# The causal mask of the score maxima, tiled by query halves: 64x64 instead of 64x128

## Chip, cores and metric

One NeuronCore of a Trainium2 chip runs the whole kernel. The metric is the device time of one execution in microseconds. The kernel before takes 1040.29 us (median of three runs, 1037.0 to 1043.07).

## What is computed

The input x has 16 sequences of 512 tokens with 128 features. Each goes through a layer-normed attention block with 16 heads of 8 features and then a mixture-of-experts feed-forward block. What matters here is the attention:

```
scores = einsum('bhqd,bhkd->bhqk', Qh, Kh)
scores = (scores + einsum('bhqd,qkd->bhqk', Qh, rel_k)) / scale   # rel_k clipped to distance 2
scores = where(causal, scores, -1e9)
attn = softmax(scores)                                            # needs the maximum of each row
out = einsum('bhqk,bhkd->bhqd', attn, Vh) + einsum('bhqk,qkd->bhqd', attn, rel_v)
```

## The kernel before

**Scores twice.** Per sequence and head the kernel forms the scores twice. In the A stage (`s_unit`, `s_part`, L1516) queries stand on the PSUM partitions and keys in the columns; VectorE takes the row maxima (`s_max`, L1127). In the B stage, one step later (`exp_unit` of TensorE, L1493), keys stand on the partitions, the maximum is already subtracted through an extra row, ScalarE applies Exp (L799), GpSimd zeroes what the causal mask forbids (L640), and TensorE multiplies with the values (`av_part`, L1553).

**Steps and rounds.** The attention is a pipeline of 19 steps over four stages: F (layer norm, queries, keys), A (maxima), B (Exp and values), C (output projection and what follows). A step has 20 rounds, r = 0 to 19, in a written order; u = r % 5 picks the shape. In a round TensorE fills two PSUM banks of scores for the maxima, one for each of two heads: `both[1]` by rows 64 to 126 of the array, `both[0]` by rows 0 to 62. With u = 0 or 3 a bank holds one query tile (n = 1, one product of 512 columns); with u = 1, 2 or 4 it holds two (n = 2; 384 + 128 or 256 + 256 columns). Banks come from a ring of three (`s_free`): VectorE reads them in the order `both[1]`, `both[0]`, and each reading frees its bank.

**The mask of the maxima.** Before VectorE may read, the diagonal 128x128 tile of each query tile needs its forbidden columns pushed down. `s_masks` (L1537) does that by products of 64 rows: `below` is a triangle of ones, `masked_at` holds -1e30 in the column that belongs to each row. It issues four matmuls a round, for two parts of the key columns (part 0: the columns of key rows 0 to 63, 64 each; part 1: 65 each) and for the two banks. All have 128 output partitions, that is the tile shape 64*128 of the array, the same as the score products around them. Half of them need the triangle's rows on the other partitions, and take them from a second, rolled copy `below_r`.

**What follows a round.** After the masks, rounds with u = 1, 2, 3 issue `av_part` (tile shape 128*32). The single products and transposes (`AT`) open rounds 1, 2, 5 to 10, 15 and 17 to 19, with shapes 128*128 or 128*32 (one of them 64*128). Only rounds 10, 15 and 19 are followed directly by the next round's score products.

**Start.** GpSimd makes the constants; `masked_columns` (L602) makes the four pieces of `masked_at` in step 0 between `split` and `near_products`. ScalarE makes `below_r` (`roll_halves`, L788). TensorE waits for both at the head of step 1, before a small product at L1741.

Of the kernel before, what the change touches and what calls it, by code (L numbers as in the profile page):

```python
# [8 lines left out]
BF16 = mybir.dt.bfloat16  # L9
U32 = mybir.dt.uint32  # L10
F32R = mybir.dt.float32r
ALU = mybir.AluOpType
# [3 lines left out]
P = 128  # L16
NSEQ, SEQ = 16, 512
# [6 lines left out]
MASKED = -1e30  # L24
HALF = P // 2
# [12 lines left out]
S_UNITS = [[(0, 3, 0)], [(0, 2, 0), (0, 0, 384)], [(0, 1, 0), (1, 1, 256)], [(1, 3, 0)], [(1, 2, 0), (1, 0, 384)]]  # L38
# [184 lines left out]
def block_kernel(nc, x, W_q, b_q, W_k, b_k, W_v, b_v, W_o, b_o, rel_k, rel_v,  # L223
                 router_w, router_bias, sw1, sw3, sw2, ew1, ew2, out):
    ctx = ExitStack()
    with ctx:  # L226
        def sb(name, shape, dt=F32):
            return ctx.enter_context(nc.sbuf_tensor(name, shape, dt))

        def sem(name):  # L230
            return ctx.enter_context(nc.semaphore(name))
# [2 lines left out]
        ident = sb("ident", [P, P])  # L234
        ident16 = sb("ident16", [P, P], F16)
        below = sb("below", [P, P], BF16)
        below_r = sb("below_r", [P, P], BF16)
        masked_at = sb("masked_at", [P, HALF + 1], BF16)
        head_sel = sb("head_sel", [P, D, NPAIR, 2])
        head_sum = sb("head_sum", [P, 32])  # L240
        wq_in = sb("wq_in", [P, P])
# [101 lines left out]
        with ExitStack() as attention:  # L343
# [34 lines left out]


        names = """  # L380
            attn_loaded qk_loaded x_loaded0 x_loaded1 x_loaded2 const_made const_ready rolled bias_full bias_ready
            m_made masked_made v_rows k_rows q_rows
            dve_own pool_own gate_own dve_own2 pool_own2 passed_sp passed_pool passed_dve passed_pe
            s_full s_free0 s_free1 s_free2 e_full e_done misc_full misc_free
# [7 lines left out]
        S = {n: sem(n) for n in names}  # L392
# [10 lines left out]
        N_CONST_MADE, N_POOL_CONST, N_QK_CONST, N_CONST = 11, 6, 6 + 6, 6 + 10  # L403
# [157 lines left out]
        def _(pool):  # L561
# [16 lines left out]
            for m in (ident, ident16):  # L578
                pool.affine_select(out=m[:, :], in_=m[:, :], compare_op=ALU.not_equal, fill=1.0, base=0,
                                   pattern=[[-1, P]], channel_multiplier=1).then_inc(S["const_ready"], 1)  # L580

            pool.affine_select(out=below[:, :], in_=below[:, :], compare_op=ALU.is_ge, fill=0.0, base=0,
                               pattern=[[-1, P]], channel_multiplier=1).then_inc(S["const_ready"], 1)

            for half in range(2):
                v = head_sel[:, :, 4 * half:4 * half + 4, :]
                pool.affine_select(out=v, in_=v, compare_op=ALU.not_equal, fill=1.0, base=-32 * half,
                                   pattern=[[-4, D], [-1, NPAIR // 2], [-64, 2]],
                                   channel_multiplier=1).then_inc(S["const_ready"], 1)

            pool.affine_select(out=m_col[:, :], in_=m_col[:, :], compare_op=ALU.not_equal, fill=-M_UNIT,
                               base=-M_ROW, pattern=[[0, 2]], channel_multiplier=1).then_inc(S["m_made"], 1)
            pool.wait_ge(S["m_made"], 1)
            pool.affine_select(out=m_col[:, :], in_=m_col[:, :], compare_op=ALU.not_equal, fill=-M_UNIT,
                               base=-M_ROW - HALF, pattern=[[0, 2]], channel_multiplier=1).then_inc(S["const_ready"], 1)

            def masked_columns():

                for i, (base, columns) in enumerate(((0, slice(0, HALF)), (-HALF, slice(0, HALF)),
                                                     (1 - HALF, slice(HALF, HALF + 1)), (1 - P, slice(HALF, HALF + 1)))):  # L600
                    v = masked_at[:, columns]
                    pool.affine_select(out=v, in_=v, compare_op=ALU.not_equal, fill=MASKED, base=base,  # L602
                                       pattern=[[-1 if i < 2 else 0, v.shape[1]]],
                                       channel_multiplier=1).then_inc(S["masked_made"], 1)
                    pool.wait_ge(S["masked_made"], i + 1)

            def selectors():

# [153 lines left out]
        def _(act):  # L762
# [19 lines left out]
                        act.dma_start(ks0[lo:lo + D, 0:NPAIR // 2, :],  # L782
                                      part[HALF * b:HALF * b + 32, :]).then_inc(stacks[0][0], 16)

            def roll_halves():

                act.wait_ge(S["const_ready"], N_POOL_CONST)
                act.copy(below_r[0:HALF, :], below[HALF:P, :]).then_inc(S["rolled"], 1)  # L788
                act.copy(below_r[HALF:P, :], below[0:HALF, :]).then_inc(S["rolled"], 1)

            def exp_unit(st, i):
                g, u, b = i // (2 * NU), i % (2 * NU) // 2, i % 2
                n, bank = st.e_use(f"e{i}")

                act.wait_ge(S["e_full"], n + 1)
                if i % (2 * NU) == 0:

                    need(act, S["av_full"], st.at(NGRP * st.b + g - 1, NGRP))
                act.activation(prob[g % 2][:, u, b, :], ps_e[bank][:, :], ACT.Exp,  # L799
                               scale=SCALE).then_inc(S["e_done"], 1)  # L800
# [94 lines left out]
            def gates_out(early):  # L895
# [9 lines left out]
                else:  # L905
                    act.wait_ge(S["gates_stored"], 32)
                    rest = (NSEQ - EARLY) * NE * NT
                    act.copy(gate_sb[0:rest, 0, :], ps_misc[0:rest, 0:P]).then_inc(S["gateT_copied"], 1)

            roll_halves()  # L910

            def step(st):
                def exps(lo, hi):
# [554 lines left out]
        def _(pe):  # L1468
# [47 lines left out]
                pe.matmul(scores[:, at:at + P * (qt + 1)], qs[par][rows, 2 * g + off, P * qt:P * qt + P],  # L1516
                          ks[par][rows, 2 * g + off, 0:P * (qt + 1)], start=(n == 0), stop=False)

            def diagonals(bank, u, part):

                n = len(S_UNITS[u])
                apart = SEQ // 2 if u == 2 else P
                if part == 0 and u != 2:
                    blocks = bank[:, SEQ - 1 - n * P:SEQ - 1].rearrange("p (n c) -> p n c", n=n)
                    return blocks[:, :, 0:HALF]
                blocks = bank[:, SEQ - n * apart:SEQ].rearrange("p (n c) -> p n c", n=n)
                at = apart - HALF - 1 if part else apart - P - 1
                return blocks[:, :, at:at + HALF + part]

            def s_masks(u, both):  # L1530

                n = len(S_UNITS[u])
                for part in range(2):
                    for b in (1, 0):
                        rows = slice(HALF * b, HALF * b + HALF)
                        columns = masked_at[rows, 0:HALF + part].unsqueeze(1).to_broadcast([HALF, n, HALF + part])
                        last = pe.matmul(diagonals(both[b], u, part), (below if b == part else below_r)[rows, :],  # L1537
                                         columns, start=False, stop=(part == 1))
                        if part == 1:
                            last.then_inc(S["s_full"], 1)  # L1540

            def av_part(st, s, g, kt):
# [68 lines left out]
            def s_tok_transpose(st):  # L1611
                m = misc(st, "s_tok")

                pe.sem_inc(passed["pe"], 1)
                transposes(lambda i: m[:, i * 64:i * 64 + 64], lambda i: s_rows[:, i * P:i * P + P],
                           ident[0:64, 0:64], S["misc_full"])
# [110 lines left out]
            def step(st):  # L1727

                uses = {"av2": lambda: av_transpose(st, st.c, 2), "e_sums": lambda: e_sums(st),
                        "m1": lambda: m_transpose(st, st.b, 1), "s_tok": lambda: s_tok_transpose(st),  # L1730
                        "av3": lambda: av_transpose(st, st.c, 3), "v0": lambda: values(st),
                        "oT": lambda: o_transpose(st), "xT": lambda: x_transpose(st), "oproj": lambda: o_proj(st),
                        "q": lambda: queries(st), "k": lambda: keys(st), "av0": lambda: av_transpose(st, st.b, 0),
                        "m0": lambda: m_transpose(st, st.a, 0), "av1": lambda: av_transpose(st, st.b, 1),
                        "xn2": lambda: xn2_transpose(st), "logits": lambda: logits(st)}
                if st.t0 == 1:
                    pe.wait_ge(S["const_ready"], N_CONST)
                    pe.wait_ge(S["rolled"], 2)
                    pe.wait_ge(S["masked_made"], 4)

                    pe.matmul(ps_av[:, 0:P], bias_v[:, :], wo[:, :], start=True, stop=True).then_inc(S["bias_full"], 1)  # L1741
                if st.t0 == 2:
                    pe.wait_ge(S["bias_ready"], 1)
                here = {"F": st.F, "A": st.A, "B": st.B, "C": st.C}
                if st.t0 == NSEQ + 2:
                    gate_transposes(True)
                for r in range(ROUNDS):
                    g, u = r // NU, r % NU
                    for what, use in uses.items():
                        if AT[what] == r and here[STAGE[what]]:  # L1750
                            if st.t0 == NSEQ + 2 and what == "xn2":
                                first_units(st)
                            use()
                    both = [None, None]

                    if st.B:
                        exp_unit(st, 2 * r)
                    if st.A:
                        both[1] = s_unit(st, 2 * r)
                    if st.B:  # L1760
                        exp_unit(st, 2 * r + 1)
                    if st.A:
                        both[0] = s_unit(st, 2 * r + 1)
                        for n in range(1, len(S_UNITS[u])):
                            for i in range(2):
                                s_part(st, 2 * r + i, both[1 - i], n)
                        s_masks(u, both)
                    for kt in {1: (0,), 2: (1, 2,), 3: (3,)}.get(u, ()):
                        if g > 0 and st.B:
                            av_part(st, st.b, g - 1, kt)  # L1770
                        if g == 0 and st.C:
                            av_part(st, st.c, NGRP - 1, kt)
# [43 lines left out]
```

## Time and profile before

| what | value |
| --- | --- |
| runs | 1037.0, 1040.29, 1043.07 us |
| profiled execution | 1038.87 us, span 1037.1 us |
| PE busy in the span | 907.4 us (87%) |
| DVE busy | 834.9 us (80%) |
| POOL, ACT busy | 726.3 us, 678.6 us |
| mean granted TensorE clock | 0.953 of 2.4 GHz |

PE is TensorE's matmuls, PEld its weight loads, DVE VectorE, ACT ScalarE, POOL GpSimd, SP the queue that issues most transfers. A matmul's record starts when it starts to stream its columns; its end is modelled and lies well after the last column, so a pause between two matmuls can be real where the records overlap. The difference of starts is what to read.

### The profile page before, as it was taken

The numbers are of one execution on the slowest core, as the hardware profiler recorded it, in microseconds if no ns is written. First come the engines' busy times: TensorE is split into PE (matmuls) and PEld (weight loads), VectorE is DVE, ScalarE is ACT, GpSimd is POOL, SyncE is SP. The second block draws the span as 40 slices with busy tenths as digits, with TensorE's granted clock in tenths as the row PEclk, the third lists the DMA queues.
The fourth block names the chain that finished last, engine by engine and source line by source line (L and its number), as shares of the span: only waits on it lengthen the run. The fifth ranks groups of instructions, "written<-read, shape, count | busy, mean of one in ns | idle before, by whom it ended". The sixth has DMA issues, their size and how long they took to land. (4 is left out here: it accounts for less than half of the span.)

```text
span 1037.1 us, 23478 instructions
## 1 busy us (share of the span) xinstructions
PE 907.4 (87%) x7655; PEld 519.9 (50%) x7655; DVE 834.9 (80%) x1948; ACT 678.6 (65%) x1305; POOL 726.3 (70%) x940
## 2 busy tenths in 40 slices
PE   2768899999999899999998999987679999999995
PEld 0324444444444444454444444432357777777773
DVE  5677878888888888888888888886568788878884
ACT  2137677767786777777867776765447767676763
POOL 4135676966867868668678686576257989898886
PEclk8569999999999999999999999998979999999999
DMA  2610111101101101011011010102415454554541
GB/s 50 168 45 28 37 39 34 51 33 41 46 32 45 43 33 48 31 43 47 32 45 43 32 49 32 42 13 57 149 58 169 143 165 151 171 148 167 162 139 31
DMA packets 64004, 74.93 MB, mean 72 GB/s; under 512 B 10032, under 2 KB 39600, under 8 KB 63904
## 3 DMA queue, kind: packets, MB, share of 16 engines
q1 hardware_dynamic: 61536, 73.17, 22.2%
q8 instruction: 56, 0.92, 0.4%
q10 hardware_dynamic: 2368, 0.48, 0.3%
q14 instruction: 44, 0.36, 0.1%
HBM read 43.75 MB, written 8.65 MB: 51 GB/s over the span
## 5 line engine op out<-in xcount | busy, mean ns | idle before, releaser
L1127 DVE TENSOR_REDUCE mx<-ps_s 128x1 f32<-128x512 f32 (+2 forms) x640 | 409.3, 684 | 82.3 <-PE ps_s L1537 80.5
L799 ACT ACTIVATE prob<-ps_e 128x512 f32<-128x512 f32 x640 | 347.8, 601 | 121.6 <-PE ps_e L1493 121.6
L640 POOL TENSOR_SCALAR_AFFINE_SELECT prob<-prob 128x516 f32<-128x516 f32 (+1 forms) x320 | 174.0, 568 | 171.3 <-ACT prob L799 171.3
L1516 PE MATMUL ps_s<-ks,qs 63*128 63x512 f16 (+3 forms) x1024 | 215.5, 311 | 20.6 <-DMA ks<-kl 8.6
L1493 PE MATMUL ps_e<-qs,ks 64*128 64x512 f16 (+3 forms) x1024 | 196.3, 304 | 15.8 <-DMA qs<-mT 7.8
L1553 PE MATMUL ps_av<-prob,vp 128*32 128x512 f32 (+3 forms) x2048 | 183.8, 455 | 22.7 <-POOL prob L640 22.4
L721 POOL TENSOR_TENSOR hidden_low<-hidden,hidden_high 128x512 fp32r<-128x512 f32 x144 | 191.2, 1356 | 12.1 <-ACT hidden_high L988 10.8
L1493 PEld LDWEIGHTS ps_e<-qs,ks 64*128 64x128 f16 x1024 | 60.9, 95 | 116.8 <-ACT prob L799 63.9
L988 ACT CAST hidden_high<-hidden 128x512 fp32r<-128x512 f32 x160 | 98.3, 614 | 30.4 <-DVE hidden L1440 25.8
L1537 PE MATMUL ps_s<-masked_at,below_r 64*128 64x130 bf16 (+3 forms) x640 | 106.5, 211 | 0.0
L1516 PEld LDWEIGHTS ps_s<-ks,qs 63*128 63x128 f16 x1024 | 63.6, 95 | 78.0 <-DVE mx L1127 54.5
L1537 PE MATMUL ps_s<-masked_at,below 64*128 64x128 bf16 (+3 forms) x640 | 92.8, 211 | 0.0
L1440 DVE TENSOR_TENSOR hidden<-gate_rows,ps_e 128x512 f32<-128x512 f32 x96 | 64.2, 684 | 28.7 <-ACT ps_e L1004 28.5
L1553 PEld LDWEIGHTS ps_av<-prob,vp 128*32 128x32 f32 x2048 | 47.3, 109 | 69.8 <-POOL prob L640 29.8
L1703 PE MATMUL ps_av<-hidden_high,w_high 128*128 128x512 f32 x160 | 69.3, 433 | 11.6 <-POOL hidden_low L721 11.6
L1004 ACT ACTIVATE ps_e<-ps_e 128x512 f32<-128x512 f32 x96 | 55.8, 582 | 20.5 <-PE ps_e L1670 19.8
L1537 PEld LDWEIGHTS ps_s<-masked_at,below_r 64*128 64x128 bf16 x640 | 60.2, 97 | 16.9 <-issue 1.6
L1703 PE MATMUL ps_av<-hidden_high,w_low 128*128 128x512 f32 x160 | 63.1, 394 | 0.0
L1703 PE MATMUL ps_av<-hidden_low,w_high 128*128 128x512 f32 x160 | 63.0, 394 | 0.0
L1537 PEld LDWEIGHTS ps_s<-masked_at,below 64*128 64x128 bf16 x640 | 53.1, 97 | 13.2 <-issue 0.5
L1561 PEld LDWEIGHTS ps_misc<-ident,av_s 128*128 128x128 f32 x256 | 28.3, 147 | 49.4 <-issue 47.2
L622 POOL TENSOR_TENSOR rs<-var,neg_half 128x4 f32<-128x4 f32 x48 | 49.1, 1024 | 3.8
(176 smaller groups left out, 1738.4 us busy)
## 6 DMA issues: line engine op xcount, KB each, us to landing
gate_rows<-gates_dram SPq DMA_DIRECT2D x128, 256.0 KB, 3.6
qs<-qh SPq DMA_DIRECT2D x128, 32.0 KB
qs<-ql SPq DMA_DIRECT2D x128, 32.0 KB
xnT_dram<-oT SPq DMA_DIRECT2D x16, 256.0 KB, 2.0
xeT<-xnT_dram SPq DMA_DIRECT2D x16, 256.0 KB, 2.7
out<-result SPq DMA_DIRECT2D x16, 256.0 KB, 2.3
v_near<-v_back SPq DMA_DIRECT2D x16, 254.0 KB
ks<-kh SPq DMA_DIRECT2D x124, 32.0 KB
```

The lines of the kernel that those rows point to most:

```text
L640: pool.affine_select(out=v, in_=v, compare_op=ALU.is_ge, fill=0.0, base=-2, pattern=cols, channel_multiplier=-1).then_inc(S["p_masked"], 1)
L721: pool.tensor_tensor(hidden_low[hid(f, i)][:, :].bitcast(F32R), hidden[hid(f, i)][:, :], hidden_high[hid(f, i)][:, :], ALU.subtract).then_ ...
L799: act.activation(prob[g % 2][:, u, b, :], ps_e[bank][:, :], ACT.Exp, scale=SCALE).then_inc(S["e_done"], 1)
L988: act.copy(hidden_high[hid(f, i)][:, :].bitcast(F32R), hidden[hid(f, i)][:, :]).then_inc(S["high_ready"], 1)
L1004: act.activation(front[k % 4][:, :], front[k % 4][:, :], ACT.Gelu).then_inc(S["act_ready"], 1)
L1127: dve.tensor_reduce(out, src, AX.X, ALU.max).then_inc(s_free[bank], 1)
L1440: dve.tensor_tensor(hidden[hid(f, i)][:, :], gate_rows[:, k, :], front[k % 4][:, :], ALU.mult).then_inc(S["hidden_ready"], 1)
L1493: last = pe.matmul(scores[:, at:at + WIDTH[kt]], ks[par][rows, pr, P * kt:P * kt + P], qs[par][rows, pr, P * kt:SEQ], start=True, stop=True)
L1516: pe.matmul(scores[:, at:at + P * (qt + 1)], qs[par][rows, 2 * g + off, P * qt:P * qt + P], ks[par][rows, 2 * g + off, 0:P * (qt + 1)], st ...
L1537: last = pe.matmul(diagonals(both[b], u, part), (below if b == part else below_r)[rows, :], columns, start=False, stop=(part == 1))
L1553: last = pe.matmul(ps_av[32 * j:32 * j + 32, P * kt:SEQ], vp[par][:, kt, 4 * g + j, :], prob[g % 2][:, u, j % 2, at:at + w], start=(kt == ...
L1703: last = pe.matmul(ps_av[:, :], ws[:, w, :].bitcast(F32R), hs[hd][:, :].bitcast(F32R), start=(i % n == 0 and j == 0), stop=(i % n == n - 1 ...
```

## The change

The four mask matmuls of a round are now cut by query halves, not by key columns. Each has 64 rows and 64 output partitions (tile shape 64*64). For the query half 64 to 127 (part 1, issued first) 65 columns a tile are written. For the half 0 to 63 (part 0) all 129 columns from the one before the tile to its last are written, 257 or 258 where the bank has two tiles. All four weights are the diagonal quadrants `below[rows, rows]`, so `below_r`, its two copies on ScalarE and the semaphore `rolled` go. `masked_at` grows from 65 to 257 columns, made by six affine selects in place of four.

```diff
-        below_r = sb("below_r", [P, P], BF16)
-        masked_at = sb("masked_at", [P, HALF + 1], BF16)
+        masked_at = sb("masked_at", [P, 2 * P + 1], BF16)
...
-                for i, (base, columns) in enumerate(((0, slice(0, HALF)), (-HALF, slice(0, HALF)),
-                                                     (1 - HALF, slice(HALF, HALF + 1)), (1 - P, slice(HALF, HALF + 1)))):
-                    v = masked_at[:, columns]
-                    pool.affine_select(out=v, in_=v, compare_op=ALU.not_equal, fill=MASKED, base=base,
-                                       pattern=[[-1 if i < 2 else 0, v.shape[1]]],
-                                       channel_multiplier=1).then_inc(S["masked_made"], 1)
-                    pool.wait_ge(S["masked_made"], i + 1)
+                blocks = masked_at[:, 1:].rearrange("p (n c) -> p n c", n=2)
+                parts = ((masked_at[:, 0:1], 0, [[0, 1]]),
+                         (blocks[:, :, 0:HALF - 1], 1, [[0, 2], [-1, HALF - 1]]),
+                         (blocks[:, :, HALF - 1:], HALF - 1, [[0, 2], [0, HALF + 1]]))
+                made = 0
+                for v, row, pattern in parts:
+                    for b in range(2):
+                        pool.affine_select(out=v, in_=v, compare_op=ALU.not_equal, fill=MASKED, base=-row - HALF * b,
+                                           pattern=pattern, channel_multiplier=1).then_inc(S["masked_made"], 1)
+                        made += 1
+                        pool.wait_ge(S["masked_made"], made)
...
-            def roll_halves():
-
-                act.wait_ge(S["const_ready"], N_POOL_CONST)
-                act.copy(below_r[0:HALF, :], below[HALF:P, :]).then_inc(S["rolled"], 1)
-                act.copy(below_r[HALF:P, :], below[0:HALF, :]).then_inc(S["rolled"], 1)
...
-                for part in range(2):
+                for part in (1, 0):
+                    queries = slice(HALF * part, HALF * part + HALF)
                     for b in (1, 0):
                         rows = slice(HALF * b, HALF * b + HALF)
-                        columns = masked_at[rows, 0:HALF + part].unsqueeze(1).to_broadcast([HALF, n, HALF + part])
-                        last = pe.matmul(diagonals(both[b], u, part), (below if b == part else below_r)[rows, :],
-                                         columns, start=False, stop=(part == 1))
-                        if part == 1:
+                        blocks = both[b][queries, SEQ - n * apart:SEQ].rearrange("p (n c) -> p n c", n=n)
+                        if part:
+                            out = blocks[:, :, apart - HALF - 1:]
+                            columns = masked_at[rows, 0:HALF + 1].unsqueeze(1).to_broadcast([HALF, n, HALF + 1])
+                        elif u == 2:
+                            out = blocks[:, :, apart - P - 1:]
+                            columns = masked_at[rows, 0:P + 1].unsqueeze(1).to_broadcast([HALF, n, P + 1])
+                        else:
+                            out, columns = both[b][queries, SEQ - n * P - 1:SEQ], masked_at[rows, 0:n * P + 1]
+                        last = pe.matmul(out, below[rows, rows], columns, start=False, stop=True)
+                        if part == 0:
                             last.then_inc(S["s_full"], 1)
...
-                    pe.wait_ge(S["rolled"], 2)
-                    pe.wait_ge(S["masked_made"], 4)
+                    pe.wait_ge(S["masked_made"], 6)
```

## Rows read from the trace of the kernel before

**Rows 1.** The page's first part: busy time of each engine, share of the span, instructions.

```profile
PE 907.4 (87%) x7655; PEld 519.9 (50%) x7655; DVE 834.9 (80%) x1948; ACT 678.6 (65%) x1305; POOL 726.3 (70%) x940
```

**Rows 2.** Busy time in four consecutive steps, 443.0 to 608.0 us, summed.

```profile
sum 165.00, PE 153.03 PEld 76.70 DVE 144.66 ACT 121.09 POOL 122.04; mean PE 38.26 PEld 19.17 DVE 36.16 ACT 30.27 POOL 30.51
```

**Rows 3.** Who waited for the mask matmuls of L1537, whole run: us, times.

```profile
  DVE mx L1127: 80.5, 116
```

**Rows 4.** Waits, 443.0 to 484.3 us (one step): engine, line, releaser: us, times, longest.

```profile
DVE mx L1127 <- PE ps_s L1537: 3.7, 7, 0.8
...
PEld ps_s L1516 <- DVE mx L1127: 3.0, 10, 0.4
...
PE ps_av L1553 <- POOL prob L640: 1.5, 2, 0.9
```

**Rows 5.** Groups by form, 200 to 600 us: the mask matmuls, n = 2, then n = 1.

```profile
L1537 PE MATMUL ps_s<-masked_at,below_r 64*128 64x130 bf16 x117 | 25.4, 217 | 0.0
...
L1537 PE MATMUL ps_s<-masked_at,below_r 64*128 64x65 bf16 x78 | 14.7, 188 | 0.0
```

**Rows 6.** Timeline of PE around a mask, n = 1: start us, us, instruction, tile, shape.

```profile
409.13 0.38 PE L1493 MATMUL ps_e<-qs,ks 64*128 64x512 f16 x1
409.34 0.19 PE L1537 MATMUL ps_s<-masked_at,below 64*128 64x64 bf16 x1
...
409.37 0.19 PE L1537 MATMUL ps_s<-masked_at,below 64*128 64x65 bf16 x1
...
409.49 0.42 PE L1553 MATMUL ps_av<-prob,vp 128*32 128x128 f32 x8
409.85 0.33 PE L1493 MATMUL ps_e<-qs,ks 64*128 64x384 f16 x1
```

**Rows 7.** Timeline of the weight loads in the same stretch.

```profile
409.12 0.10 PEld L1537 LDWEIGHTS ps_s<-masked_at,below 64*128 64x128 bf16 x1
...
409.49 0.16 PEld L1553 LDWEIGHTS ps_av<-prob,vp 128*32 128x32 f32 x8
```

**Rows 8.** Timeline of PE from round 19 into round 0 of the next step.

```profile
484.12 0.22 PE L1537 MATMUL ps_s<-masked_at,below 64*128 64x130 bf16 x1
484.16 0.37 PE L1493 MATMUL ps_e<-qs,ks 64*128 64x512 f16 x1
...
485.12 0.39 PE L1516 MATMUL ps_s<-ks,qs 63*128 63x512 f16 x1
485.12 0.20 PE L1537 MATMUL ps_s<-masked_at,below_r 64*128 64x64 bf16 x1
...
485.38 0.19 PE L1537 MATMUL ps_s<-masked_at,below_r 64*128 64x65 bf16 x1
```

**Rows 9.** Timeline of PE in round 4, n = 2.

```profile
451.79 0.22 PE L1537 MATMUL ps_s<-masked_at,below 64*128 64x130 bf16 x1
...
451.95 0.22 PE L1537 MATMUL ps_s<-masked_at,below_r 64*128 64x130 bf16 x1
452.10 0.39 PE L1561 MATMUL ps_misc<-ident,m 128*8 128x128 f16 x4
```

**Rows 10.** Timeline of DVE, rounds 18 and 19 (in brackets idle before, releaser).

```profile
482.36 1.29 DVE L1127 TENSOR_REDUCE mx<-ps_s 128x1 f32<-128x512 f32 x2 [0.15 <-PE ps_s L1537]
...
484.37 1.91 DVE L1127 TENSOR_REDUCE mx<-ps_s 128x4 f32<-128x512 f32 x3 [0.72 <-PE ps_s L1537]
```

**Rows 11.** Timeline of PE: the queries of round 9, and the values after round 16.

```profile
461.62 1.13 PE L1576 MATMUL ps_e<-xnT,wq 128*128 128x512 f32 x2
...
477.08 1.06 PE L1553 MATMUL ps_av<-prob,vp 128*32 128x512 f32 x8 [0.87 <-POOL prob L640]
```

**Rows 12.** Start of the kernel: POOL's timeline.

```profile
19.29 1.29 POOL L602 TENSOR_SCALAR_AFFINE_SELECT masked_at<-masked_at 128x64 bf16<-128x64 bf16 x4
```

**Rows 13.** Waits, 0 to 90 us.

```profile
PE ps_s L1516 <- DMA ks<-kl: 8.6, 2, 8.3
...
PE ps_av L1741 <- POOL masked_at L602: 5.1, 1, 5.1
```

More of the change, by code:

```diff
@@ L380, in block_kernel @@
         names = """
-            attn_loaded qk_loaded x_loaded0 x_loaded1 x_loaded2 const_made const_ready rolled bias_full bias_ready
+            attn_loaded qk_loaded x_loaded0 x_loaded1 x_loaded2 const_made const_ready bias_full bias_ready
             m_made masked_made v_rows k_rows q_rows
@@ L908, in gates_out @@
                     act.copy(gate_sb[0:rest, 0, :], ps_misc[0:rest, 0:P]).then_inc(S["gateT_copied"], 1)
-            roll_halves()
             def step(st):
@@ L1517, in s_part, with s_masks @@
                           ks[par][rows, 2 * g + off, 0:P * (qt + 1)], start=(n == 0), stop=False)
-            def diagonals(bank, u, part):
+            def s_masks(u, both):
                 n = len(S_UNITS[u])
                 apart = SEQ // 2 if u == 2 else P
[L1523 to L1532, printed above, removed]
-                for part in range(2):
+                for part in (1, 0):
+                    queries = slice(HALF * part, HALF * part + HALF)
                     for b in (1, 0):
                         rows = slice(HALF * b, HALF * b + HALF)
-                        columns = masked_at[rows, 0:HALF + part].unsqueeze(1).to_broadcast([HALF, n, HALF + part])
-                        last = pe.matmul(diagonals(both[b], u, part), (below if b == part else below_r)[rows, :],
-                                         columns, start=False, stop=(part == 1))
-                        if part == 1:
+                        blocks = both[b][queries, SEQ - n * apart:SEQ].rearrange("p (n c) -> p n c", n=n)
[9 more added lines that the diff above has]
+                        if part == 0:
                             last.then_inc(S["s_full"], 1)
```

## The prediction

> **What bounds the kernel now.** I read the page's busy times first, then the busy time by stretches, the waits, and last the timeline of single rounds. TensorE is busy for 87% of the span and VectorE for 80% [rows 1]; the mask runs only in the attention, whose middle repeats in steps of 165.00 / 4 = 41.3 us with TensorE busy 38.3 and VectorE 36.2 [rows 2]. Neither is full, and each waits for the other: in one step VectorE waits 7 times, 3.7 us in all, for a mask, and the score products wait 10 times, 3.0 us, for VectorE to free a bank [rows 4]. Over the run VectorE waits 116 times for a mask [rows 3], about 7 in each of the 16 steps that have one. So the end is set by a chain that changes between the two, and the last thing TensorE does before handing over is exactly what is changed.
>
> **Columns.** Two matmuls on different row halves run side by side: in a round with n = 1 the mask pairs start at 409.34 and 409.37 [rows 6]. A column takes 1/2.4 ns (512 of them lie between 409.13 and 409.34 [rows 6]). Before, each row half streams 64 + 65 = 129 columns (54 ns) with n = 1 and 128 + 130 = 258 (107 ns) with n = 2 [rows 5]. After, the longer of the two query halves streams 129 and 257 or 258. If both column halves of the array run side by side, too, as the four 128*32 tiles do (eight matmuls of 128 two-pass columns in 0.42 us, where in a row they would need 8 x 0.107 = 0.85 us [rows 6]), the time is the same: 0. If they run one after the other, it is 27 ns a round more for n = 1 and 54 for n = 2. I take 0.
>
> **The change of tile shape.** This is the term that counts. Score products and masks share the shape 64*128. Between them there is no pause: the mask starts at 409.34, when the 512 columns end, its weights loaded at 409.12 under the products [rows 6, 7]; and from round 19 to 0 the next product starts at 484.16, before the 130 columns of 484.12 have ended [rows 8]. Where the shape changes, there is a pause each time: the last mask at 409.37 has streamed by 409.40, and the 128*32 tiles begin at 409.49, their weights at 409.49 too, not earlier [rows 6, 7]; in round 4 the last mask, 451.95 + 0.05, is followed at 452.10 [rows 9]. That is 0.09 to 0.10 us in which nothing is loaded ahead. No row shows 64*128 followed by 64*64. Bounds: 0, if a mere column split of the same row halves isn't a new shape; 0.12, the pause with a first weight load exposed. Between 64*128 and 128*8 both dimensions differ, so the rows alone leave this open; I take 0.09, because every change in the rows shows it.
>
> Here the Trainium skill has a rule: TensorEngine Tiling (Array Packing), Key Properties, says that changing the tiling mode, not just the tile, drains the engine, and the section Tiling Modes lists 64×128 and 64×64 as different modes. The pauses of 0.09 to 0.10 us agree with a drain. By it the pause is sure and the lower bound of 0 falls away.
>
> To the entry comes the first weight load, which is no longer hidden. The nearest row is the 128*32 block: 0.42 us less two times 0.107 of columns and less the modelled tail of 0.16 (a 64-column mask has 0.19 for 0.03 of columns) leaves 0.04, some 0.02 of it the stagger of eight starts [rows 6]. So 0.02, between 0 and 0.04.
>
> The same skill page, Restrictions and Gotchas, says that column tiling disables the fast weight load. By it, and by the page TensorE: Matmul & The Clock Gate, section LDWEIGHTS (columns over 1.2 GHz), the 64 columns of a mask would take an estimated 53 ns, and each entry 0.03 us more than I take; no run here shows it.
>
> One mask block then costs 0.09 + 0.02 = 0.11 us on entry. On exit 17 of the 20 rounds change shape already; in rounds 10, 15 and 19 the product that now starts at once (484.16 [rows 8]) gets a second pause of 0.09. TensorE's own bill is 20 x 0.11 + 3 x 0.09 = 2.5 us a step, 40 us for 16 steps: the upper bound for side-by-side columns.
>
> **How much of it reaches the end.** I follow one step's waits.
> - Rounds 17 to 19: TensorE leads, VectorE waits before 482.36 (0.15 us) and 484.37 (0.72 us) [rows 10], and once in round 17. Three blocks, all exposed.
> - Rounds 0 and 1: VectorE works without a pause (three reductions from 484.37), and one would say that it covers TensorE. But the bank of `both[0]` is free only after the first reduction, 484.37 + 0.68 = 485.05; its product starts at 485.12 [rows 8, 10]. Before, the masks of `both[1]` ran beside that product (485.12 [rows 8]) and were early. Now all masks wait until the product has drained: 485.12 + 0.21 + 0.11 + 0.05 = 485.49, and VectorE starts 0.20 after the last mask (484.12 + 0.05 to 484.37), at 485.69. It would be free at 484.37 + 2 x 0.61 = 485.59 (reductions start 0.61 apart: 1.91 less 1.29 [rows 10]). So the cover is gone and some 0.1 us is exposed here as well.
> - Rounds 2 to 8: the score products wait for VectorE and VectorE again for masks, in turn, several of the 7 and 10 waits of [rows 4]. Seven blocks, exposed at about 0.11 each.
> - Rounds 9 to 16: from the queries' product at 461.62 a longer chain runs over ScalarE's Exp and GpSimd's masking, and TensorE stands idle 0.87 us before 477.08 [rows 4, 11]. Eight entries and two exits, 8 x 0.11 + 2 x 0.09 = 1.06 us, find 0.87 of cover; 0.2 is left.
> Sum: 12 blocks x 0.11 = 1.3, and 0.2, makes 1.5 us a step; x 16 = 24 us.
>
> **The rest.** The two copies of `below_r` go from ScalarE's start, the affine selects become six, by the four of 1.29 us about 0.65 more, up to 1 us, as they are wider [rows 12]. Behind them on GpSimd stand the `near_products` of step 0, and TensorE's small product waits for them (5.1 us [rows 13]). But after it TensorE waits 8.3 us for the keys' transfers [rows 13], which neither of these moves. 0; with that cover gone, +1. The feed-forward part isn't touched.
>
> The profiled execution takes 1038.87 us; 1038.87 + 24 = 1063. The median of the runs is 1.4 above it. I forecast 1064 us.
>
> **The rivals.**
> - *VectorE covers most* (0.13). The shape costs what I say, but is exposed only where VectorE waits for a mask now: 7 x 0.11 x 16 = 12 us, 1052. For it: VectorE has work queued in rounds 0 to 7. Against: the bank cycle above.
> - *The column halves also stream one after the other, or the weight load is slow* (0.14). Extra 8 x 27 + 12 x 54 ns = 0.86 us a step; on 12 of 20 rounds 0.5 us, x 16 = 8 us, 1072; with everything exposed 40 + 14 = 54 us, 1094. For it: in no row are there two 64-wide column tiles. Against: the 128*32 tiles.
> - *No pause between 64*128 and 64*64* (0.10), the other side. The masks cost the same columns, the shape costs nothing on entry, and four quadrants load less: half the weight columns. Price: 0, or a gain up to 15 ns a block, 320 x 0.015 = 5 us where the loads were late; 1035 to 1041. It decides if the mask block starts when the last product's columns end. For it: only row changes may matter. Against: a pause at every change of shape in the trace. That the change doesn't do what it says would look the same, 1040.
> - My own forecast has 0.63, its own range 1054 to 1075.
>
> **Numbers.** About 0.5% (5 us) is what can be told from no change. The slower cases are 0.63 + 0.13 + 0.14 = 0.90; the no-pause case divides into 0.06 same and 0.04 faster. The range 1049 to 1081 leaves out the no-pause case and the extreme of the second rival.
>
> **What would show it.** Right: 64*64 masks starting about 0.09 us after the products' last column, with their loads not earlier; all four within 0.03 us of each other; no mask beside a product of the other bank; in rounds 10, 15 and 19 a pause before the next product; a step of 42.8 us; VectorE waiting more often, rounds 0 and 1 included; the idle time before 477.08 nearly gone. Wrong: masks that begin at once (no pause), column halves that start 0.05 to 0.11 us apart (second rival), or a step that grows by under 0.9 us though the pause is there (first rival).

## The result and the profile after

The changed kernel takes 1072.28 us (median of four runs, 1056.98 to 1075.88) against 1041.68. The ratio is 1.023, with a 95% interval of 1.018 to 1.028; it counts the two slowest runs of the changed kernel, 1074.09 and 1075.88 us, as slow ones and leaves them out, and so lies below the ratio of the medians, 1.029. In a second comparison it was 1069.99 us (six runs) against 1038.70 (eleven), ratio 1.029, 1.027 to 1.032. The profiled execution took 1070.47 us; its span is 1068.8, 31.7 more than before.

The page's first part and its row of granted clock, by slices of the span:

```profile
PE 966.5 (90%) x7655; PEld 500.5 (47%) x7655; DVE 840.2 (79%) x1948; ACT 680.6 (64%) x1303; POOL 725.2 (68%) x942
...
PEclk8569999999998898988989889898879999999999
```

TensorE is busier by 59 us with the same number of matmuls, its weight loads by 19 us less, and the other engines are within 6 us of before [rows 1]. And there is something the prediction does not mention: through the attention the row of the clock is broken by 8s.

**The pause.** The timeline of PE after the change in round 18 (n = 1), to be held against [rows 6], and of its weight loads, against [rows 7]:

```profile
409.74 0.38 PE L1488 MATMUL ps_e<-qs,ks 64*128 64x512 f16 x1
410.05 0.25 PE L1531 MATMUL ps_s<-masked_at,below 64*64 64x65 bf16 x4
410.23 0.43 PE L1546 MATMUL ps_av<-prob,vp 128*32 128x128 f32 x8
```

```profile
410.05 0.11 PEld L1531 LDWEIGHTS ps_s<-masked_at,below 64*64 64x64 bf16 x4 [0.43 <-issue]
410.23 0.16 PEld L1546 LDWEIGHTS ps_av<-prob,vp 128*32 128x32 f32 x8
```

The 512 columns end at 409.74 + 0.21 = 409.95 and the masks start at 410.05, their weights loaded then and not under the products. The pause is there. The four masks start within 0.03 us of each other (the four records span 0.25 us). From the masks to the 128*32 tiles it is 0.18 us. The 129 columns take 0.05 of it. With two tiles in a bank, here in round 19, it is 0.24 us, of which the longer half's 257 columns take 0.11 (the row names the other half's 130):

```profile
238.26 0.30 PE L1531 MATMUL ps_s<-masked_at,below 64*64 64x130 bf16 x4
238.50 0.39 PE L1488 MATMUL ps_e<-qs,ks 64*128 64x512 f16 x1
```

Both times 0.13 us is left beside the longer half's columns, though the columns double. If the column halves streamed one after the other, the remainder would be 0.10 and 0.08. So they run side by side. The 0.13 holds the stagger of the four starts, the pause and some 0.025 us more than on leaving a 64*128 block. I put this 0.025 down to the masks' first weight load, which no row shows by itself.

**The step.** A step is read from VectorE's first reduction of round 19 to the next such one. The kernel before has it at 484.37 us [rows 10], and one step earlier at 443.06, which makes a step of 41.31 us:

```profile
443.06 0.69 DVE L1127 TENSOR_REDUCE mx<-ps_s 128x4 f32<-128x512 f32 x1 [0.72 <-PE ps_s L1537]
```

In the changed kernel these are the rows at the two ends of a step at full clock, and of one later in the run:

```profile
238.60 0.69 DVE L1122 TENSOR_REDUCE mx<-ps_s 128x4 f32<-128x512 f32 x1 [0.84 <-PE ps_s L1531]
...
281.13 2.04 DVE L1122 TENSOR_REDUCE mx<-ps_s 128x4 f32<-128x512 f32 x3 [0.84 <-PE ps_s L1531]
...
457.39 1.29 DVE L1122 TENSOR_REDUCE mx<-ps_s 128x4 f32<-128x512 f32 x2 [1.39 <-PE ps_s L1531]
...
501.77 1.29 DVE L1122 TENSOR_REDUCE mx<-ps_s 128x4 f32<-128x512 f32 x2 [1.39 <-PE ps_s L1531]
```

The first two are 42.53 us apart, 1.22 more than before; the last two 44.38. The three reductions that took 1.91 us without a pause [rows 10] now take 2.04: the 0.13 us is the gap in round 0 that the prediction expected, because a bank is freed too late. The 44.38 has another cause, shown by the busy time and granted clock (the number before the DMA share) in stretches cut at the changes of the clock:

```profile
core 0: us, PE busy (x) PEld busy (x) DVE busy (x) ACT busy (x) POOL busy (x), PEclk, DMA share, GB/s
...
329.60:367.10 37.50, 36.08 (x372) 16.08 (x364) 31.50 (x78) 26.22 (x51) 26.11 (x37) 1.00 0.10 34
367.10:373.90 6.80, 6.80 (x42) 2.15 (x45) 4.81 (x14) 4.13 (x11) 4.38 (x9) 0.50 0.15 51
373.90:411.40 37.50, 36.09 (x372) 15.99 (x364) 31.52 (x78) 26.23 (x51) 26.01 (x37) 1.00 0.10 34
411.50:418.30 6.80, 6.80 (x42) 2.15 (x45) 4.81 (x14) 4.13 (x11) 4.38 (x9) 0.50 0.14 50
```

From 322.8 us on the clock falls to 1.2 GHz for 6.8 us in every step, always from round 19 to the values behind round 1, each time costing 44.38 - 42.53 = 1.85 us. There are nine such falls in the attention's steps, about 17 us. The kernel before had one fall of 3.4 us in the same stretch.

The rest can be counted in steps. In both kernels the third of these reductions comes at nearly the same time, and the last one 13 steps later, first before and then after the change:

```profile
153.65 1.91 DVE L1127 TENSOR_REDUCE mx<-ps_s 128x4 f32<-128x512 f32 x3 [0.72 <-PE ps_s L1537]
...
688.79 1.29 DVE L1127 TENSOR_REDUCE mx<-ps_s 128x4 f32<-128x512 f32 x2 [0.72 <-PE ps_s L1537]
```

```profile
153.27 2.04 DVE L1122 TENSOR_REDUCE mx<-ps_s 128x4 f32<-128x512 f32 x3 [0.84 <-PE ps_s L1531]
...
721.32 1.29 DVE L1122 TENSOR_REDUCE mx<-ps_s 128x4 f32<-128x512 f32 x2 [0.84 <-PE ps_s L1531]
```

That is 535.1 against 568.1 us: 32.9 more, of which 13 x 1.22 = 16 are the pauses and 17 the clock. So the growth of the span alone would mislead: the two shares have to be told apart. And up to 153 us the changed kernel lost nothing in these two executions, though it had the pauses there as well. The kernel before had three falls of the clock of 3.4 us between 80 and 150 us, the changed kernel one; whether that is the whole reason was not tried.

### The profile page after: what moved, and what is told of

It reads as the page before. It is cut to its first block and busy times, and to the rows that moved or that the text cites. A ratio compares the mean times of both kernels' runs of the same rounds, so it can differ in the third digit from the quotient of the medians.

```text
span 1068.8 us, 23480 instructions
## 1 busy us (share of the span) xinstructions
PE 966.5 (90%) x7655; PEld 500.5 (47%) x7655; DVE 840.2 (79%) x1948; ACT 680.6 (64%) x1303; POOL 725.2 (68%) x942
## 5 line engine op out<-in xcount | busy, mean ns | idle before, releaser
L1122 DVE TENSOR_REDUCE mx<-ps_s 128x1 f32<-128x512 f32 (+2 forms) x640 | 414.0, 683 | 104.1 <-PE ps_s L1531 95.9
L1511 PE MATMUL ps_s<-ks,qs 63*128 63x512 f16 (+3 forms) x1024 | 227.0, 323 | 20.6 <-DVE mx L1122 9.3
L1488 PE MATMUL ps_e<-qs,ks 64*128 64x512 f16 (+3 forms) x1024 | 204.3, 317 | 6.5 <-DMA qs<-mT 3.4
L1511 PEld LDWEIGHTS ps_s<-ks,qs 63*128 63x128 f16 x1024 | 67.0, 97 | 89.1 <-DVE mx L1122 62.9
L1531 PE MATMUL ps_s<-masked_at,below 64*64 64x130 bf16 (+4 forms) x1280 | 95.2, 263 | 0.0
L1531 PEld LDWEIGHTS ps_s<-masked_at,below 64*64 64x64 bf16 x1280 | 37.1, 106 | 89.9 <-issue 87.3
L1554 PE MATMUL ps_misc<-ident,av_s 128*128 128x128 f32 x256 | 43.3, 294 | 4.0 <-ACT av_s L861 3.9
L1696 PEld LDWEIGHTS ps_av<-hidden_high,w_high 128*128 128x128 f32 x160 | 30.3, 189 | 31.3 <-POOL hidden_low L724 27.2
```

Of the source, the lines that this page charges most:

```text
L1122: dve.tensor_reduce(out, src, AX.X, ALU.max).then_inc(s_free[bank], 1)
L1488: last = pe.matmul(scores[:, at:at + WIDTH[kt]], ks[par][rows, pr, P * kt:P * kt + P], qs[par][rows, pr, P * kt:SEQ], start=True, stop=True)
L1531: last = pe.matmul(out, below[rows, rows], columns, start=False, stop=True)
L1554: last = pe.transpose(dst(i), src(i), unit)
L1696: last = pe.matmul(ps_av[:, :], ws[:, w, :].bitcast(F32R), hs[hd][:, :].bitcast(F32R), start=(i % n == 0 and j == 0), stop=(i % n == n - 1 ...
```

## The experiments

Steps below are read as above, at full clock where not said. Every ratio is against the kernel before, run beside it: 1038.70 us in experiments 1 to 3, 1040.82 in 4, 5 and the first of 6, 1039.76 in the second of 6 and in 7. Experiments 1 to 3 ran on one chip, 4 to 7 on another.

**1. The changed kernel again, six runs.**

> The changed kernel itself, to see how its time goes with the clock. Theory A (two costs: a pause at each change of tile shape, and TensorE's clock falling to 1.2 GHz for 6.8 us in most steps): runs in which the clock stays at 2.4 GHz take about 1057 us at a mean clock of 0.95, runs with the falls 1070 to 1076 at 0.93. Theory B (the clock has no part, all of the loss is the pauses): the time doesn't go with the clock.

Measured (us at mean granted clock): 1063.83 at 0.949, 1064.04 at 0.950, 1069.54 at 0.928, 1070.45 at 0.929, 1071.03 at 0.926, 1073.45 at 0.923; the four runs of the first comparison: 1056.98 at 0.952, 1070.47 at 0.929, 1074.09 at 0.925, 1075.88 at 0.931. On the whole the time goes with the clock, which speaks for theory A and against B. But at a mean clock of 0.95 this set took 1064, not the expected 1057: the profile of the run with 1064.04 us shows seven of the falls of 6.8 us, where that of the first comparison has nine.

**2. 64*64 masks in a part of the rounds.** Both kinds of mask are kept, and the round chooses:

```diff
-                        s_masks(u, both)
+                        (s_masks_new if 9 <= r <= 16 else s_masks_old)(u, both)
```

(in the second run `not 9 <= r <= 16`)

> 64*64 masks in rounds 9 to 16 alone, 64*128 in the others (below_r kept, masked_at made by six selects). By the prediction's split the idle time before the values of round 16 covers them: +0.2 us a step, +3 us, 1043 to 1045. If every pause counts (rival): 8 x 0.11 + 2 x 0.09 = 1.06 a step, +17 us, 1057.

> 64*64 masks in rounds 17 to 19 and 0 to 8 alone. By the prediction 12 x 0.11 = 1.3 us a step, +21 us, about 1061, without a fall of the clock; if VectorE covered rounds 0 to 8, 3 x 0.11 x 16 = +5, 1046. If the clock falls here too, up to 1072; that would place its cause in these rounds.

Rounds 9 to 16 alone: 1046.14 us, ratio 1.007 (1.005 to 1.009), little falling of the clock. The others alone: 1057.68, ratio 1.018 (1.014 to 1.021), with falls in some steps. Two consecutive steps of each, at full clock:

```profile
486.29 1.91 DVE L1131 TENSOR_REDUCE mx<-ps_s 128x4 f32<-128x512 f32 x3 [0.72 <-PE ps_s L1541]
...
528.24 1.90 DVE L1131 TENSOR_REDUCE mx<-ps_s 128x4 f32<-128x512 f32 x3 [0.71 <-PE ps_s L1541]
```

```profile
280.53 2.04 DVE L1131 TENSOR_REDUCE mx<-ps_s 128x4 f32<-128x512 f32 x3 [0.84 <-PE ps_s L1563]
...
322.53 2.04 DVE L1131 TENSOR_REDUCE mx<-ps_s 128x4 f32<-128x512 f32 x3 [0.84 <-PE ps_s L1563]
```

41.95 and 42.00: +0.64 and +0.69 a step. Together they make 1.33, near the change's whole 1.22, but the split is not the predicted one of 0.2 and 1.3. Rounds 9 to 16 cost three times as much, the others half.

**3. Half of the columns.** The query half 0 to 63 also gets 65 columns a tile, so that the longer column half streams half of what it did. The kernel then leaves out the mask of the key columns 64 to 127 for these queries.

```diff
-                        elif u == 2:
-                            out = blocks[:, :, apart - P - 1:]
-                            columns = masked_at[rows, 0:P + 1].unsqueeze(1).to_broadcast([HALF, n, P + 1])
                         else:
-                            out, columns = both[b][queries, SEQ - n * P - 1:SEQ], masked_at[rows, 0:n * P + 1]
+                            at = apart - P - 1 if u == 2 else apart - HALF - 1
+                            out = blocks[:, :, at:at + HALF + 1]
+                            columns = masked_at[rows, 0:HALF + 1].unsqueeze(1).to_broadcast([HALF, n, HALF + 1])
```

> The changed kernel with only 65 columns a tile for the query half 0 to 63 as well (the upper key half stays unmasked, left out on purpose of cost): same 1280 matmuls, same shapes, half of the mask's columns. If the shape is the cost, the steps shorten by at most the columns, 27 ns (n = 1) or 54 ns (n = 2) a round, 0.4 to 0.9 us a step, and remain over the kernel before by 0.5 us or more a step; if the columns are the cost (the rival of halves one after the other), the step falls to about that of before, 41.3.

1052.61 us, ratio 1.014 (1.011 to 1.017); steps of 42.18 us (reductions at 534.32 and 576.50). With half the columns the masks in 64*64 still cost 0.87 us a step over the kernel before. So most of the cost is the shape's; halving the columns gives back 0.35 us a step of the 1.22.

**4. Each bank's masks behind its own products.** The same edit on both kernels (`s_masks` gets the banks as a third argument; that part is not shown):

```diff
                     if st.A:
                         both[1] = s_unit(st, 2 * r)
+                        for n in range(1, len(S_UNITS[u])):
+                            s_part(st, 2 * r, both[1], n)
+                        s_masks(u, both, (1,))
                     if st.B:
                         exp_unit(st, 2 * r + 1)
                     if st.A:
                         both[0] = s_unit(st, 2 * r + 1)
                         for n in range(1, len(S_UNITS[u])):
-                            for i in range(2):
-                                s_part(st, 2 * r + i, both[1 - i], n)
-                        s_masks(u, both)
+                            s_part(st, 2 * r + 1, both[0], n)
+                        s_masks(u, both, (0,))
```

> The kernel before with each bank's two masks issued right behind its own score products, before the other bank's products; all shapes stay 64*128. No shape changes are added; the order alone changes: 1036 to 1044 by the theory of pauses.

> The same order with the 64*64 masks: two entries and two exits a round instead of one. To be read against bank_128. Per round 2 entries of 0.09 and a weight load of 0.025 each, and one more exit of 0.12: 0.35 us, 7.0 a step, of which at least half is exposed (as 1.2 of 2.5 was in the changed kernel): 3.5 to 7 us a step, 56 to 110 over bank_128, about 1095 to 1150. If the pause were paid for the columns or the weights and not for the change of shape, the time would be that of the changed kernel, 1057 to 1075.

With 64*128 masks: 1035.15 us, ratio 0.994 (0.993 to 0.996), steps of 40.90. That is a version faster than both kernels. With 64*64: 1079.94, ratio 1.038 (1.035 to 1.041), steps of 43.46. The same masks, in the same order, differ by 45 us through their shape alone. The expectation of 56 to 110 us was too high: it took half or more of 7.0 us a step to be exposed, and 2.56 were. What covers the rest was not followed. The rival in which the number of changes of shape doesn't matter is out: a step is 0.93 us longer than in the changed kernel. Round 0 of bank_64, then of bank_128, on PE:

```profile
429.91 0.39 PE L1488 MATMUL ps_e<-qs,ks 64*128 64x512 f16 x1
...
430.23 0.24 PE L1531 MATMUL ps_s<-masked_at,below 64*64 64x65 bf16 x2
430.41 0.39 PE L1488 MATMUL ps_e<-qs,ks 64*128 64x512 f16 x1
...
430.73 0.24 PE L1531 MATMUL ps_s<-masked_at,below 64*64 64x65 bf16 x2
```

```profile
440.13 0.37 PE L1516 MATMUL ps_s<-ks,qs 63*128 63x512 f16 x1
440.34 0.19 PE L1537 MATMUL ps_s<-masked_at,below_r 64*128 64x64 bf16 x1
440.38 0.19 PE L1537 MATMUL ps_s<-masked_at,below 64*128 64x65 bf16 x1
440.39 0.39 PE L1516 MATMUL ps_s<-ks,qs 63*128 63x512 f16 x1
440.40 0.38 PE L1493 MATMUL ps_e<-qs,ks 64*128 64x512 f16 x1
```

From products to masks: 430.23 - 429.91 - 0.21 = 0.11 us of pause; back: 430.41 - 430.23 - 0.05 = 0.13. In 64*128 the masks start 0.21 after the product, without a pause, and the next product 0.01 behind them, on the other row half.

**5. Fewer changes of shape in the kernel before.**

```diff
-                    for kt in {1: (0,), 2: (1, 2,), 3: (3,)}.get(u, ()):
+                    for kt in {2: (0, 1, 2,), 3: (3,)}.get(u, ()):
```

> The kernel before with the values' first part (kt = 0) moved from the rounds with u = 1 to those with u = 2, beside the other two parts: four blocks of shape 128*32 a step fewer, five changes of shape less (each 0.09 to 0.10 us), and the wait for GpSimd in rounds 1 and 16 gone. If a change of shape costs what it does in the trace: 0.25 to 0.5 us a step less, 1030 to 1036; if the longer block of round u = 2 is in the way of the Exp products (rival), 1040 to 1050.

1082.28 us, ratio 1.040 (1.038 to 1.043). The expected gain is missed; it came out on the rival's side, and far past its 1050. The values now run in blocks of 24 tiles, on PE:

```profile
440.69 2.14 PE L1553 MATMUL ps_av<-prob,vp 128*32 128x512 f32 x24
```

In an 83 us window of this run the score products' weight loads wait 14.5 us for VectorE and VectorE 12.7 us for masks, where the kernel before has 5.4 and 9.3. That the long block is what parts them I take from these waits; the experiment moves the block and takes the changes of shape away together and says nothing on the price of one.

**6. Work in front of the idle time.** In the changed kernel the Exp products of one round are issued twice into the same bank:

```diff
-                for off, kt, at in E_UNITS[u]:
+                for off, kt, at in E_UNITS[u] * (2 if i // 2 == 17 else 1):
```

> The changed kernel with the Exp products of round 17 issued twice into the same bank (same result; 8 products of 256 columns for 4, some 0.2 to 0.4 us of TensorE more a step, placed before its idle 0.7 us ahead of round 18). If TensorE's idleness there is what lets the clock fall one round later (theory A), the falls go or become rare: mean clock 0.95 or more, steps of 42.5 to 42.8 us, 1057 to 1062. If the falls have another cause, clock 0.925 to 0.93 and 1070 to 1078.

> Control to twice_17: the same number of doubled Exp products, but in round 12, where TensorE waits 0.4 us for VectorE and which lies 5 rounds and over 9 us before the place where the clock falls. If it is the idleness ahead of round 18 that lets the clock fall, the falls stay: mean clock 0.925 to 0.95, steps of 44.4 us among them, 1064 to 1073. If any additional work anywhere holds the clock, it is as with twice_17: 0.96, 1053 to 1058.

Doubled in round 17: 1055.67 us (1052.67 to 1057.92), ratio 1.015 (1.012 to 1.018), clock 0.951 to 0.969. More work makes the kernel 14 us faster than it was in experiment 1. That was on another chip; the ratios, 1.015 and 1.029, say the same. Its profile has a single fall, of 3.4 us, between 160 and 700 us. Doubled in round 12: 1064.08 (1058.16 to 1069.95), ratio 1.023 (1.019 to 1.026), clock 0.929 to 0.957. In its profile seven falls of 6.8 us remain in the attention's steps, as many as in the profile of experiment 1. Steps of twice_17, then of twice_12, from VectorE's rows:

```profile
366.95 2.04 DVE L1122 TENSOR_REDUCE mx<-ps_s 128x4 f32<-128x512 f32 x3 [0.84 <-PE ps_s L1531]
...
409.50 2.04 DVE L1122 TENSOR_REDUCE mx<-ps_s 128x4 f32<-128x512 f32 x3 [0.84 <-PE ps_s L1531]
```

```profile
369.93 1.29 DVE L1122 TENSOR_REDUCE mx<-ps_s 128x4 f32<-128x512 f32 x2 [1.39 <-PE ps_s L1531]
...
414.34 1.29 DVE L1122 TENSOR_REDUCE mx<-ps_s 128x4 f32<-128x512 f32 x2 [1.41 <-PE ps_s L1531]
```

42.55 against 44.41. So the falls are a cost of their own, which four products in the right place take away. The place counts for the most part, though round 12 may help a little as well (1064 against 1070, ranges overlapping). At 42.55 us a step the pauses stand nearly alone: 1055.67 is 15 to 16 us over the kernel before.

**7. The start alone.**

```diff
-        masked_at = sb("masked_at", [P, HALF + 1], BF16)
+        masked_at = sb("masked_at", [P, 2 * P + 1], BF16)
...
```

(with the six selects of the change and the wait for them; the masks as before)

> The kernel before, with masked_at widened to 257 columns and made by six affine selects; its masks read the first 65 columns, which hold the same values, and below_r stays. By the prediction the start is covered by the keys' transfers: within 1 us of the kernel before, 1038 to 1042. If the start carries a part of the loss: 1 us or more over it.

1040.37 us, ratio 1.0005 (0.999 to 1.002). GpSimd's timeline shows what is covered:

```profile
19.43 2.32 POOL L606 TENSOR_SCALAR_AFFINE_SELECT masked_at<-masked_at 128x1 bf16<-128x1 bf16 x6
```

1.0 us more than the four of [rows 12], at the upper end of the estimate, and it costs nothing. That the two copies of `below_r` cost nothing was not tried by itself.

## Why the prediction was right, and where it was not

The direction, the mechanism of the pause and the range were right (1064 forecast, 1049 to 1081; 1072.28 measured, 1069.99 in the repeat). That the number comes so near is in part luck: the sum had the pauses 8 us too high, 24 for 16, and the clock's 17 us not at all.

- *The pause at a change of shape.* Predicted 0.09 on entry, 0.02 for the weight load. Measured 0.09 to 0.10, and 0.025 more on leaving the block. The bound of 0 for 64*128 to 64*64 is out: shown by the timeline, by half_columns and by the pair bank_128 and bank_64. Every row here agrees with the drain that the Trainium skill states (TensorEngine Tiling (Array Packing), Key Properties), also for a change of the column tiling alone (0.09 to 0.10 us from 64*128 to 64*64).
- *The weight load.* The estimate of 53 ns, worked out from the Trainium skill (TensorEngine Tiling (Array Packing), Restrictions and Gotchas, and TensorE: Matmul & The Clock Gate, section LDWEIGHTS), did not come: all that is left for the first load is 0.025 us.
- *Columns side by side, 0.* Right: the four start within 0.03 us, and leaving the block takes as long beside 129 columns as beside 257. The rival of halves one after the other is out.
- *TensorE's own bill, 2.5 us a step,* was not measured as such; of it 1.22 us reached the end at full clock, where 1.5 was predicted. A step was to be 42.8 and was 42.53. The 1.22 lies between this and the 0.77 (7 x 0.11) of the rival in which VectorE covers most.
- *"x 16".* In the two profiled executions the 1.22 added up in 13 steps only; up to 153 us nothing was lost. Of the 8 us, 16 x 0.28 = 4.5 come from the step and 3 x 1.22 = 3.7 from the count.
- *Rounds 9 to 16, "0.87 of cover; 0.2 is left".* This step failed: 0.64 was exposed. In the changed kernel the idle time before the values of round 16 did go: TensorE's 128*32 block at 230.51 us shows no wait. But behind it another chain had become late. The waits of POOL, 200 to 600 us, before and then after:

```profile
POOL var L619 <- DVE mv L1090: 0.4, 1, 0.4
```

```profile
POOL var L622 <- DVE mv L1085: 7.1, 9, 1.0
```

  and on PE in round 18, before and then after:

```profile
481.06 0.66 PE L1561 MATMUL ps_misc<-ident,y 128*128 128x128 f32 x4 [0.45 <-DVE num L1178]
```

```profile
235.09 0.63 PE L1554 MATMUL ps_misc<-ident,y 128*128 128x128 f32 x4 [0.80 <-POOL y L627]
```

  VectorE's statistics for the layer norm stand in its queue behind the reductions of rounds 12 to 15, which the pauses delay. GpSimd's norm waits for them (7.1 us in nine steps, where it was 0.4 in one). TensorE waits 0.6 to 0.8 us for its result, where it waited 0.45 for VectorE. With the new masks in rounds 9 to 16 alone (one step of experiment 2) TensorE's two longest waits are:

```profile
PE ps_av L1578 <- POOL prob L644: 0.9, 1, 0.9
PE ps_misc L1586 <- POOL y L628: 0.9, 1, 0.9
```

  The first stands in round 1; the one of round 16 is gone. The second is 0.41 longer than the 0.45 of before, and with the 0.2 left it makes 0.6, near the 0.64 measured. The wait of round 1 grew as well, from 0.63 to 0.87, and smaller ones shrank; I did not follow every one. With the new masks in the other rounds alone TensorE has no wait for `y`, so this chain belongs to rounds 9 to 16. I had counted the cover on one engine only; the work hidden behind it passes through VectorE.
- *Rounds 17 to 19 and 0 to 8, twelve blocks at 0.11.* Too large: 0.69 was exposed instead of 1.3, though the gap in round 0 came (0.13 us). The prediction overlooked a second cover. The kernel before stands 0.63 us for GpSimd in round 1 (the other of the two waits for `prob` in [rows 4]); after the change 0.39 is left:

```profile
487.85 1.07 PE L1553 MATMUL ps_av<-prob,vp 128*32 128x512 f32 x8 [0.63 <-POOL prob L640]
```

```profile
242.08 1.07 PE L1546 MATMUL ps_av<-prob,vp 128*32 128x512 f32 x8 [0.39 <-POOL prob L643]
```

  With the new masks in these rounds alone only the wait of round 16 is left in a step, and that of round 1 is gone:

```profile
PE ps_av L1578 <- POOL prob L644: 0.8, 1, 0.8
```

  1.3 less 0.63 is about the 0.69 measured; the small waits were not followed here either. The sum had two small slips as well, which work against each other: it took two blocks for rounds 0 and 1 where its reading gave 0.1 for both, and it left out the exit of round 19, 0.09.
- *The clock* was in no term. It is worth about 17 us of the profiled execution (nine falls) and about 13 of the one in experiment 1 (seven), and on the whole the slower runs of the changed kernel are those with the lower clock: they spread over 19 us where those of before spread over 6. Without the falls the forecast would have been 8 us too high. The rival in which VectorE covers most (1052) is nearer to the pauses alone, 1055 to 1057, than my forecast was.
- *The start, 0.* Right (experiment 7).

## What to carry to other kernels

Cutting a matmul into smaller array tiles beside products of another tile shape buys no streaming time where the longer part streams as many columns as before, and here it cost a pause of 0.09 to 0.12 us each time the shape changes, in which nothing is loaded ahead. Keep neighbours in one shape; within it, issuing each bank's masks right behind its own products was worth 0.6% here. Where an idle time is to cover a delay, list all idle times of the step, ask of each engine that feeds the end of one whether it is delayed as well, and look at the granted clock by step before charging a difference to instructions.

## What the runs showed that was not expected

- With row halves of one shape TensorE starts a matmul of one half while an earlier one of the other half still waits. In the kernel before, round 4, a mask starts at 451.73, and the product of the other bank, which the program issues ahead of it, at 451.84:

```profile
451.73 0.22 PE L1537 MATMUL ps_s<-masked_at,below_r 64*128 64x128 bf16 x1
...
451.84 0.22 PE L1516 MATMUL ps_s<-ks,qs 63*128 63x128 f16 x1
```

  The change of shape takes that away, too: in the changed kernel a mask block starts 0.09 to 0.10 us after the last column of the products of both halves.
- The clock fell once per step, 44.4 us apart, though TensorE was busier than in the kernel before, in which it hardly fell: 36.09 of the 37.5 us ahead of the fall at 411.5, 96%, against 93% in [rows 2]. Four more products before the idle 0.8 us of round 18 held it up. Why the kernel before, which waits 0.87 us in round 16 and 0.45 in round 18, does not lose it stays open; busy time, whose ends are modelled, does not tell.
